# An attention and mixture-of-experts layer on one core: two blocks' query transfers split between two issuing engines, and one mask moved on VectorE

## The reference

```python
q, k, v = silu(x @ Wq), silu(x @ Wk), x @ Wv            # 16 heads of 8
q, k = lrpe(q), lrpe(k)                                 # times cos and sin of an angle per position
energy = einsum('bhnd,bhmd->bhnm', q, k) * tril         # the mask multiplies
out = einsum('bhnm,bhmd->bhnd', energy, v) @ Wo * sigmoid(x @ G1 @ G2)
x1 = layernorm(x + (layernorm(out) * gamma + beta))     # the first and the second norm
routed = experts_of_top_2(x1)
out = layernorm(x1 + shared(x1) + routed)
```

## Time and profile before

| what | value |
|---|---|
| runs | 825.44, 819.38, 820.43 us |
| median | 820.43 us |
| span of the profiled execution | 819.0 us |
| busy share PE, DVE, POOL, ACT | 94%, 71%, 51%, 45% |
| chain that ended last | PE 78%, DVE 10%, issue 4%, DMA 3%, SP's queue 2%, POOL 2% |

### The profile page before, as it was taken

The page is one execution under the profiler, slowest core; times in us unless marked ns, Lnnn a source line. Parts: engine busy times, 40 slices in busy tenths (PEclk is TensorE's granted clock), DMA queues, the critical chain, the costliest instruction groups (busy, mean ns, idle before and its releaser), DMA issues.

```text
span 819.0 us, 30731 instructions
## 1 busy us (share of the span) xinstructions
PE 771.5 (94%) x12462; PEld 627.2 (77%) x12462; DVE 583.9 (71%) x1865; ACT 368.2 (45%) x802; POOL 415.7 (51%) x395
## 2 busy tenths in 40 slices
PE   5889999999999999999998889899999999999994
PEld 4667777777777777778776677688999989899884
DVE  7488798888888888898868898845444454544674
ACT  6334564646546465564633332223322333323484
POOL 6441243523435243342534555671677778876442
PEclk9999999999999999999999999999999999999997
DMA  4155233231333323233322212114444455433455
GB/s 148 46 174 180 78 92 85 64 93 53 100 76 78 90 57 97 61 86 77 77 64 54 69 34 70 42 53 137 98 87 58 80 98 102 72 52 42 126 151 145
DMA packets 71163, 70.56 MB, mean 86 GB/s; under 512 B 11443, under 2 KB 54250, under 8 KB 71024
## 3 DMA queue, kind: packets, MB, share of 16 engines
q1 hardware_dynamic: 53928, 52.33, 23.2%
q0 software_dynamic: 17024, 16.28, 11.0%
q10 hardware_dynamic: 72, 0.00, 0.0%
HBM read 23.99 MB, written 28.89 MB: 65 GB/s over the span
## 4 chain that ended last, share of the span: by engine, by line
PE 78%; DVE 10%; issue 4%; DMA 3%; SPq 2%; POOL 2%; ACT 1%; POOLq 0%; DVEq 0%; ACTq 0%
PE energy_banks L1935 5%; PE bank L1853 5%; PE energy_and_gate_banks L1853 5%; PE bank L1855 5%; PE bank L1854 5%; PE energy_and_gate_banks L2409 4%; PE bank L2409 4%; PE energy_and_gate_banks L1960 4%; PE energy_and_gate_banks L1855 3%; PE energy_and_gate_banks L1854 3%; PE bank L1894 3%; PE energy_banks L1853 3%; PE energy_banks L1855 3%; PE energy_banks L1854 3%; PE bank L1895 2%
## 5 line engine op out<-in xcount | busy, mean ns | idle before, releaser
L626 POOL DMA_INDIRECT dispatched_rows<-x,slot x128 | 140.0, 1093 | 224.5 <-PE energy_banks L1935 132.4
L760 POOL DMA_INDIRECT summed_rows<-VP,goal_i x80 | 123.8, 1548 | 42.5 <-issue 22.7
L1119 ACT ACTIVATE sq<-energy_banks 128x512 f32<-128x512 f32 (+1 forms) x96 | 50.5, 526 | 120.2 <-PE energy_banks L1855 118.5
L842 ACT ACTIVATE hidden_rounded<-sf 128x512 fp32r<-128x512 f32 x88 | 55.3, 628 | 58.8 <-DVE sf L1273 58.0
L832 ACT ACTIVATE sf<-energy_and_gate_banks 128x512 f32<-128x512 f32 x88 | 52.4, 596 | 62.2 <-PE energy_and_gate_banks L1855 60.8
L1273 DVE TENSOR_TENSOR sf<-sf,bank 128x512 f32<-128x512 f32 x88 | 60.1, 683 | 19.4 <-PE bank L1855 19.2
L1935 PE MATMUL energy_banks<-EM,VP 64*32 64x64 f32 x4096 | 59.1, 225 | 1.1 <-issue 1.1
L1243 DVE TENSOR_TENSOR EM<-energy_and_gate_banks,causal 128x512 f32<-128x512 f32 x64 | 43.9, 686 | 18.7 <-PE energy_banks L1960 18.7
L1853 PE MATMUL energy_and_gate_banks<-xgT_hi,ws_hi 128*128 128x512 f32 x108 | 52.1, 482 | 3.4 <-DVE EM L1243 2.6
L1935 PEld LDWEIGHTS energy_banks<-EM,VP 64*32 64x32 f32 x4096 | 47.8, 105 | 4.2 <-issue 3.2
L1853 PE MATMUL bank<-xgT_hi,ws_hi 128*128 128x512 f32 x108 | 45.9, 425 | 3.7 <-DVE sf L1273 1.4
(11 more groups left out here) (255 smaller groups left out, 2178.4 us busy)
## 6 DMA issues: line engine op xcount, KB each, us to landing
QM<-QT SPq DMA_DIRECT2D x248, 32.0 KB
dispatched_rows<-empty POOLq DMA_DIRECT2D x8, 655.0 KB
QM<-dispatched_rows SPq DMA_DIRECT2D x8, 655.0 KB, 6.2
QT<-sq SPq DMA_DIRECT2D x40, 128.0 KB
KT<-sq SPq DMA_DIRECT2D x40, 128.0 KB
xin<-in_x SPq DMA_DIRECT2D x16, 256.0 KB, 2.9
QM<-summed_rows SPq DMA_DIRECT2D x16, 256.0 KB, 2.8
out_x<-QM SPq DMA_DIRECT2D x16, 256.0 KB, 3.2
```

Source lines behind the costliest of these rows:

```text
L626: g.indirect_dma_start(out=xg_d, out_offset=bass.IndirectOffsetOnAxis(ap=slot[:, n % 2, j:j + 1], axis=0), in_=x1[:, n % 2, j % NC, :], in ...
L760: g.indirect_dma_start(out=sum_d, out_offset=bass.IndirectOffsetOnAxis(ap=goal_i[:, par, t:t + 1], axis=0), in_=ye[:, par, t, :], in_offse ...
L842: a.activation(hs_hi[:, f], sf[:, n % SF], ACT.Copy).then_inc(a_hh, 1)
```

## The change

The two lists of issues for blocks 1 and 2 are divided as block 0's already was: SP issues heads 0 to 3 of each half (`range(4 if b < 2 else 8)`), POOL heads 4 to 7 (`upper_heads`). For block 1 POOL does so at the end of step 0, behind the two weight splits; for block 2 in step 1, one half behind the third fill, the other behind the fourth and ahead of `rr`. The counts that others wait for follow. On DVE the mask of chunk 3 of block 1 (in block 0 nothing stands between the two places) goes ahead of `second_moments` and `mean_square`.

```diff
         def loads_of_q(b):
-            return P * b + P // 2 if b >= 0 else 0
+            if b < 0:
+                return 0
+            return P // 2 * (b + 1) if b < 3 else P * b - P // 2
+
+        def half_loads_of_q(b):
+            return P // 2 * (b + 1)
...
                     need(sp, pe_kt, 2 * (f - 2) + 2)
-                    need(sp, g_qm[0], loads_of_q(f - 2))
-                    need(sp, g_qm[1], loads_of_q(f - 2))
+                    for g2 in (0, 1):
+                        need(sp, g_qm[g2], loads_of_q(f - 2))
+                        if f < 5:
+                            need(sp, g_q0[g2], half_loads_of_q(f - 2))
...
                         need(sp, pe_E, 8 * b + 4 * g2 + 4)
-                        for h in range(4 if b == -1 else 8):
+                        for h in range(4 if b < 2 else 8):
                             q_by_head(sp, 1 - par, g2, h, g_qm[g2])
...
+                def upper_heads(g2):
+                    need(gp, v_qk, 4 * f + 2)
+                    need(gp, pe_E, 8 * b + 4 * g2 + 4)
+                    for h in range(4, 8):
+                        q_by_head(gp, 1 - par, g2, h, g_q0[g2])
                 if b in (1, 2):
                     gp.wait_ge(c_pool, 25)
                     gp.wait_ge(g_qm[1], loads_of_q(b))
+                    gp.wait_ge(g_q0[1], half_loads_of_q(b))
...
                     fill(4 * b - 2)
+                    if b == 1:
+                        upper_heads(0)
                     need(gp, pe_av, 4 * b + 3)
                     fill(4 * b - 1)
+                    if b == 1:
+                        upper_heads(1)
...
                         split_shared(i)
+                    upper_heads(0)
+                    upper_heads(1)
...
                     mask_state(b, 6)
+                    mask(b, par, 3)
                     if back:
                         second_moments(b)
                         mean_square(b)
-                    mask(b, par, 3)
...
-                        if b == 0:
-                            need(pe, g_q0[c // 2], P // 2)
+                        if b < 3:
+                            need(pe, g_q0[c // 2], half_loads_of_q(b))
```

## The result

The changed kernel took 824.55 us (median of 22 runs, 820.23 to 828.7), the kernel before beside it 821.01 us (22 runs, 818.51 to 826.57): ratio 1.0037, 95% interval [1.0019, 1.0054]. By the ratio that is 3.0 us slower, by the medians 3.5, where 0.3 us faster was forecast, and it lies over the top of the range (822.9). It is within 1%, as expected with 0.96.

A forecast was written before the change was run, and what follows sets the result against it. PE was taken as the bound (busy 94% of the span), with DVE once waiting for a doubling that SP issued late. -0.89 + 0.55 = -0.34 us, from the median 820.43, gave 820.1 us; range 817.5 to 822.9.

The forecast's parts named there:

- the prices of the issues: Transfers issued by POOL cost 0.52 us each, those by SP 0.87 us; POOL's last four end before `rr`.
- that SP would wait: Step 1: SP is through with block 2's queries near 58.4 us, then waits for POOL's `input_and_bias` before block 3's input.
- the mask gives PE nothing ahead of `input_lo`: Step 2: the mask starts 1.1 us earlier, but PE's projection of block 3 stays at 59.2 us.
- `scale_x1` is blocked by `input_and_bias`: DVE's scaling ends its wait only at 61.35 us, so `mask(2, 0)` starts at 62.55 instead of 62.00: +0.55 us.
- the -0.89 us for the wait for the doubling: DVE's idle time before block 3's angles, near 72.04 us, goes because SP issues the doubling earlier: 0.89 us gained.
- if DVE still waits for the doubling, SP was not what made it late: Sign of a wrong forecast: idle time left on DVE before block 3's first angles, expected at 71.7 us without any.
- A gain on the side: POOL's first fill and weight split move ahead some 2 us, sparing DVE a 1.4 us stall; nothing at the end.
- about +1: TensorE's lower clock lasting 2 us longer than before costs about 1 us; placed on the slower side.
- the slower case: POOL's four issues before `rr` take over 0.87 us each, or the lower clock lasts longer: 821 to 822.8 us, chance 0.18.
- cost and gain nothing for PE: Start of step 2: the mask's 1.1 us are given back at once, as the statistics only change places with it.
- The sum -0.89 + 0.55: The doubling's wait gone, `mask(2, 0)` later: -0.34 us in all, carried to the end of the span; chance 0.45.
- the better case: `mask(2, 0)` stays at 62.00, or TensorE's clock also stays at 2.4 GHz: 818.5 to 819.5 us, chance 0.22.

The follow-up runs named there:

- the fifth: The changed kernel with the second and third fill of step 1 held back: 822.72 us, ratio 1.0033 to the kernel before.
- the eighth experiment: The kernel before with one edit, block 1's first reciprocal root put behind the third fill, which is issued earlier: 821.46 us, ratio 1.0005.

## Why the prediction was wrong

- **Right: the prices of the issues, and that SP would wait.** POOL's issues cost 0.49 us each (0.52 in the forecast) and their last ended before `rr`; SP was through at 59.0 (58.4) and waited for `input_and_bias`. That 59.0 is near 58.4 is partly luck: the last energies ended 1.5 us later than forecast, at 56.42, and SP's four issues behind them took 0.62 us each, not 0.87.
- **Right: the mask gives PE nothing ahead of `input_lo`** (with the mask alone the projection stays at 59.18), **and `scale_x1` is blocked by `input_and_bias`:** its four instructions took 2.06 us, and 1.12 with that collision removed (the row before has 1.14, the forecast reckoned with 1.05). The Trainium skill, SBUF — State Buffer, section Who interferes with whom, has the rule; the trace agrees, for a form that the step 3 row had not shown. It is not the mask's price alone: with the split alone the scaling took 2.06 us too, since `rr` there starts right behind POOL's last issue, at 59.08.
- **Wrong: the -0.89 us for the wait for the doubling.** The split was to bring the doubling forward. SP's wait for `input_and_bias` took 3.8 us and ate the 2.8 us that SP had won, so the doubling was issued 0.93 us later than before. DVE met no wait because it came 0.79 us later itself (72.83 against 72.04). By the prediction's own sign, "if DVE still waits for the doubling, SP was not what made it late": with the split alone DVE still waits 0.94 us, in the one profile there is.
- **Wrong: "A gain on the side", costed at nothing for the end.** I saw that POOL's fills move ahead and asked only what that spares DVE, not what the transfers would stand in front of. An instruction packet comes late, and PE waits 1.95 us before 54.70. Behind it the profile is 1.1 to 1.5 us later than the forecast. Against the copy of the kernel before it is 0.96 us late in step 3 and 1.47 in step 12, which is the order's whole cost and takes in the blocked scaling.
- **Wrong, and the larger part as far as the runs tell: the clock, "about +1", on the side of the slower case.** I wrote that the gap of 2.03 us "is not closed, it is cut into one of 0.9 and one of 1.4 us", and used this only against a gain. The profile had the warning: 59 to 61 us at 0.56, behind that gap. With four gaps of 0.66 to 1.43 us the stretch behind them falls to 1.2 GHz in more executions. What the extra products gave back was 2.8 us (the control in step 1 gave back nothing); the same products gave the kernel before 0.0006, so the change's own share is about 0.0028, 2.3 us, uncertain by about 2.7 us (the intervals together). That term belonged into the sum, not at the edge of a rival with 0.18. The mask's move, "cost and gain nothing for PE", costs 1.7 us (0.0021 of 820.8, interval 0.6 to 2.9 us), which is gone when PE is kept busy.
- **The sum -0.89 + 0.55** treated a wait on DVE as time at the end. DVE's start on block 3's angles lay between 71.2 and 76.8 in the profiles of these kernels without the median following: the changed kernel with the products in step 2 had it at 74.83 and a median of 819.62 us, the mask alone at 71.22 and 822.60.
- **The range** allowed 1 us of scatter under the better case and none over the slower one, though a cause that sets in only in some executions belongs in a median's upper end.

Open: why the clock falls in one execution and not in the next, and how the 3 us divide between clock and order to better than a microsecond. The profiled execution of the changed kernel was busy for 4.71 of 8 us and kept 2.4 GHz; the runs list a mean clock only, so the share of executions that lose it in step 2 was not measured.

## What to carry to other kernels

Where TensorE bounds the kernel, add up its idle time in each stretch of some microseconds, before and after a change; to cut one gap into several is not neutral, and the granted clock of the stretch behind shows what is at stake. If the runs list a mean clock, compare it beside looking for a late wait: here it went with half or more of the difference, and one profile of a fast execution hid it. But cycles that are not granted while TensorE has no work cost nothing, so a mean clock is a hint and not a price. Products that nobody reads, put into such gaps, are a quick test of a clock theory, with the same products elsewhere as the control. A transfer that starts earlier for free may stand in front of another one, probably an engine's instructions included. And before relieving an engine that issues late, ask what its next entries wait for: here two other waits took over at once.

## What the runs showed of the hardware that was not expected

The traces show an "instruction" queue that shares the DMA engines with the data: one packet of 0.02 MB about every 4 us in this stretch, late at 52.2 instead of 50.6 us when a fill of 655 KB was issued 1.6 us earlier. In five of the seven profiles with an early fill PE then has an unnamed wait of 1.4 to 2.7 us between 49 and 55 us (1.2 and 0.6 us in the other two); in the two of the unchanged kernel the longest there is 0.6 and 0.9 us. That the packet is PE's is inferred: it moved with the gap, both ways, in the fifth and the eighth experiment.

Work that nobody reads may make the kernel before faster too: seven products of 512 columns in a gap of 2.03 us gave 0.998 [0.9958, 1.0002], and the mean clock rose from 0.990 to 0.993. The Trainium skill, TensorE: Matmul & The Clock Gate, section Part 1 (The HAM clock gate), says that the clock is one of two levels and follows how busy TensorE has been; the stretches at 0.50 and at 1.00 agree with the two levels. The fourteen products agree with the rest: in step 2 they raise the mean clock to 0.994, and in step 1, where no profile shows the lower level, they leave it at 0.987.
